# Six of the eight passes' inputs turned by VectorE blocks and SBUF transfers instead of by TensorE

## The chip, the cores and the metric

One NeuronCore of a Trainium2 chip runs the whole program. The metric is the device time of one execution in microseconds; the median of three runs stands for a kernel. TensorE (PE), VectorE (DVE), ScalarE (ACT), GpSimd (POOL) and SyncE (SP) each run their own instructions in order and meet at semaphores. SP issues all of the kernel's DMA transfers.

## What is computed

```python
# x: 4 x 512 tokens x 512
x = x + 0.5 * L0_ffn(layernorm(x))     # W1, W3: 2048 x 512; silu(x W1') * (x W3'), Hadamard, W2
x = x + L0_attn(layernorm(x))          # layernorm again, causal attention, residual
x = x + 0.5 * L0_ffn(layernorm(x))
x = x + 0.5 * L1_ffn(layernorm(x))     # ternary gate, up, down: 1408 x 512, with scales
x = x + L1_attn(layernorm(x))          # tanh(x B') C' + D * x
x = x + 0.5 * L1_ffn(layernorm(x))
```

Each feed-forward layer takes the normalised activations with the 512 features on the partitions, so the rows (tokens on the partitions) that the layernorm gives have to be transposed first: 128 tokens x 512 features at a time, a *tile*.

## The kernel before

**Passes.** The four feed-forward layers run as eight passes over half of the tokens each (two chunks of 512 tokens, eight tiles): passes 0 and 1, attention, 2 and 3 (kind A, 16 units of 128 hidden features), 4 and 5, the state-space layer, 6 and 7 (kind B, ternary, 11 units). Each pass is a row of slots, one slot for one unit. Within a slot the up products go by a seven-product scheme (p1 to p7) over sums of quarters of the input, xc_hi and xc_lo; the quarters themselves lie in xs. Every fp32 matmul is done as three with split high and low parts (`three`), or as two in the ternary passes, whose weights have no low part.

**A slot on PE** (`run`, `first_half`, `second_half`): in kind A p1, p5, p6, p2, then four down tiles, then the turns, then p7, p3, p4. In kind B p1 of slot s + 1 is done in slot s, ahead of p3 or behind it, then p4; slot s + 1 begins with p5, p6, p2, its down tiles, the turns. p6 adds onto bank BY, which `seed_y` on ACT fills; ACT may do so once DVE has read the slot before's BY in `sum_c22`. The down tiles read hid, the last block of which goes `gated_first` (DVE) -> `hid_high` (ACT) -> `low` (DVE).

**The turns** (`turn_tiles`, L997) make the input of the *next* pass in four slots of each pass: ACT normalises two tiles into xn in the slots `NORMS` (`norm_pair`, L1452; four tiles of room), one slot later PE transposes each of the two in four 128 x 128 pieces through the identity into a PSUM bank, and ACT copies the banks to xs (`turn_out`, L1300). Six passes do so (0, 2, 3, 4, 5, 6); pass 1 feeds attention and goes its own way, and pass 7 feeds nothing. Near a pass's end DVE forms the sums of the quarters (`sums`, L2053) once all eight tiles are `turned`.

**SP's order** is written out by hand. For kind A a slot issues: the next unit's up weights (`w13_load`, L579, which waits for p4 of the slot before), then a block of down weights (`w2_load`, L612). For kind B: the later parts and the low half of the next unit's up weights, which wait for p4 of the slot before; a block of down weights; then, when p6 and p2 of this slot are done, the first part of the unit after it.

**DVE's order** in a slot of kind B (`ternary_slot`, L2338): a down tile added to y (`add_tile`), `seed_z`, further down tiles and the items of `extra`, then `sum_c22` (waits for ACT's `seed_w`, hence for p7), `gated_second`, `gated_first` (waits for p4), two `hid_low`.

## Time and profile before

| | |
|---|---|
| median of 3 runs | 1706.19 us (1705.47 to 1707.06) |
| span of the profiled execution | 1703.6 us |
| PE busy | 1694.7 us, 99% |
| DVE, ACT, POOL busy | 1154.4, 830.3, 125.5 us |
| granted clock | 0.9 or more of full speed in all 40 slices |
| chain that ended last | PE 94% |
| DMA | 344.56 MB, 97341 packets |

The profiled execution's only time is its span, 2.6 us under the median of the timed runs: what lies around the program is not in it. A slot is best cut at the starts of ACT's `seed_y` (L1423), one in each unit; times within a slot of kind B are counted below from the moment at which p4 of the slot before is done, which SP's first weight load of the slot marks.

### The profile page before, as it was taken

The numbers are of one execution on the slowest core, as the hardware profiler recorded it, in microseconds if no ns is written. First come the engines' busy times: TensorE is split into PE (matmuls) and PEld (weight loads), VectorE is DVE, ScalarE is ACT, GpSimd is POOL, SyncE is SP. The second block draws the span as 40 slices with busy tenths as digits, with TensorE's granted clock in tenths as the row PEclk, the third lists the DMA queues.
The fourth block names the chain that finished last, engine by engine and source line by source line (L and its number), as shares of the span: only waits on it lengthen the run. The fifth ranks groups of instructions, "written<-read, shape, count | busy, mean of one in ns | idle before, by whom it ended". The sixth has DMA issues, their size and how long they took to land.

```text
span 1703.6 us, 21742 instructions
## 1 busy us (share of the span) xinstructions
PE 1694.7 (99%) x7707; PEld 1401.8 (82%) x7707; DVE 1154.4 (68%) x1808; ACT 830.3 (49%) x1359; POOL 125.5 (7%) x185
## 2 busy tenths in 40 slices
PE   9999999999999999999999999999999999999998
PEld 7788888888888888888888888888888888888887
DVE  8888678677775555754446554447768869877866
ACT  5745444465575543434223333224556556655644
POOL 1000000000012220000000000000000143200001
PEclk9999999999999999999999999999999999999999
DMA  9776665699985000253444433444666763366765
GB/s 317 266 310 247 229 258 211 236 377 369 369 333 207 1 0 1 87 191 126 153 167 167 167 142 136 167 167 146 232 215 211 273 222 112 113 242 234 257 221 213
DMA packets 97341, 344.56 MB, mean 202 GB/s; under 512 B 10192, under 2 KB 25424, under 8 KB 91856
## 3 DMA queue, kind: packets, MB, share of 16 engines
q1 hardware_dynamic: 97232, 343.14, 55.0%
q8 instruction: 65, 1.06, 0.2%
q14 instruction: 44, 0.36, 0.1%
HBM read 261.83 MB, written 81.26 MB: 201 GB/s over the span
## 4 chain that ended last, share of the span: by engine, by line
PE 94%; DVE 3%; DMA 1%; SPq 1%; issue 1%; ACT 0%; DVEq 0%; ACTq 0%
PE psum L561 35%; PE psum L563 30%; PE psum L565 27%; PE psum L857 2%; DMA x<-in_w2a 1%; SPq L705 1%; DVE xc_lo L2074 0%; DMA flat<-in_w3a 0%; DMA w<-w_kept 0%; PE psum L1134 0%; DVE att_lo L2043 0%; DVE fw_lo L2037 0%; SPq L664 0%; DVE x L2020 0%; DVE x L2123 0%
## 5 line engine op out<-in xcount | busy, mean ns | idle before, releaser
L561 PE MATMUL psum<-xc_hi,w 128*128 128x512 f32 x1544 | 604.6, 392 | 0.5 <-DVE psum L2143 0.3
L563 PE MATMUL psum<-xc_lo,w 128*128 128x512 f32 x1544 | 600.9, 389 | 0.0
L565 PE MATMUL psum<-xc_hi,w 128*128 128x512 f32 x928 | 361.3, 389 | 0.0
L561 PEld LDWEIGHTS psum<-xc_hi,w 128*128 128x128 f32 x1544 | 289.8, 188 | 64.4 <-DVE psum L2143 1.6
L563 PEld LDWEIGHTS psum<-xc_lo,w 128*128 128x128 f32 x1544 | 289.9, 188 | 58.8
L561 PE MATMUL psum<-w,hid 128*128 128x512 f32 x864 | 337.5, 391 | 0.0
L565 PE MATMUL psum<-w,hid 128*128 128x512 f32 x864 | 336.4, 389 | 0.0
L2107 DVE TENSOR_TENSOR x<-psum,x 128x512 f32<-128x512 f32 x256 | 173.0, 687 | 148.3 <-PE psum L565 147.7
L563 PE MATMUL psum<-w,hid 128*128 128x512 f32 x544 | 211.7, 389 | 0.0
L565 PEld LDWEIGHTS psum<-xc_hi,w 128*128 128x128 f32 x928 | 174.2, 188 | 36.7
L2131 DVE TENSOR_TENSOR hid<-sg,hid 128x512 fp32r<-128x512 f32 x212 | 144.3, 691 | 85.2 <-ACT hid L1450 83.3
L561 PEld LDWEIGHTS psum<-w,hid 128*128 128x128 f32 x864 | 162.2, 188 | 36.1 <-DVE x L2107 2.7
L565 PEld LDWEIGHTS psum<-w,hid 128*128 128x128 f32 x864 | 162.2, 188 | 33.9
L1480 ACT ACTIVATE psum<-psum 128x512 f32<-128x512 f32 x108 | 62.9, 582 | 237.6 <-PE psum L565 172.4
L1450 ACT ACTIVATE hid<-sg 128x512 fp32r<-128x512 f32 x204 | 125.6, 627 | 105.1 <-DVE sg L2156 51.9
L2147 DVE TENSOR_TENSOR sg<-psum,sg 128x512 f32<-128x512 f32 x104 | 71.6, 688 | 91.1 <-ACT psum L1480 90.7
L563 PEld LDWEIGHTS psum<-w,hid 128*128 128x128 f32 x544 | 102.2, 188 | 20.4
L2143 DVE TENSOR_TENSOR psum<-psum,sg 128x512 f32<-128x512 f32 x104 | 72.2, 694 | 43.8 <-PE psum L565 36.9
L1423 ACT ACTIVATE psum<-psum 128x512 f32<-128x512 f32 x108 | 62.8, 581 | 79.9 <-PE psum L565 54.7
L1884 POOL TENSOR_SCALAR var_eps<-meanvar 128x4 f32<-128x4 f32 x24 | 7.0, 290 | 1242.1 <-DVE meanvar L1988 865.1
L1472 ACT ACTIVATE sg<-psum 128x512 f32<-128x512 f32 x64 | 38.0, 593 | 89.2 <-PE psum L565 89.2
L1298 ACT ACTIVATE xn<-x,shift,rstd 128x512 f32<-128x512 f32 x88 | 65.7, 807 | 13.0 <-POOL shift L1887 9.9
(177 smaller groups left out, 2030.1 us busy)
## 6 DMA issues: line engine op xcount, KB each, us to landing
w<-w_kept SPq DMA_DIRECT2D x93, 896.0 KB, 6.6
w<-w_kept SPq DMA_DIRECT2D x130, 512.0 KB, 7.1
w<-w_kept SPq DMA_DIRECT2D x57, 640.0 KB, 4.4
w_kept<-w SPq DMA_DIRECT2D x16, 1792.0 KB, 7.3
w<-w_kept SPq DMA_DIRECT2D x93, 256.0 KB, 4.5
w_kept<-prep SPq DMA_DIRECT2D x12, 1792.0 KB, 7.6
w_kept<-w SPq DMA_DIRECT2D x16, 512.0 KB, 6.3
w_kept<-prep SPq DMA_DIRECT2D x12, 512.0 KB, 8.9
```

Of the source, the lines that this page charges most:

```text
L561: pe.matmul(out, a_hi, b_hi, start=start, stop=False, skip_group_check=onto)
L563: last = pe.matmul(out, a_hi, b_lo, start=False, stop=stop and zero == "a", skip_group_check=onto)
L565: last = pe.matmul(out, a_lo, b_hi, start=False, stop=stop, skip_group_check=onto)
L1298: return copy(out, x[:, i, :], AF.Identity, bias=shift[:, i:i + 1], scale=rstd[:, i:i + 1])
L1423: copy(bank(BY), bank(BX), AF.Copy).then_inc(y_seeded, 1)
L1450: copy(hid_of(u, c)[:, 0, :], own(u) if c else sg[:, 0, :], AF.Copy).then_inc(hid_hi_ready, 1)
L1472: copy(sg[:, 0, :], bank(BX), AF.Silu, scale=gate_scale(ps, s)).then_inc(c11_read, 1)
L1480: copy(bank(BW), bank(BY), AF.Copy).then_inc(w_seeded, 1)
L2107: tt(at_x, b, at_x, ALU.add).then_inc(added, 1)
L2131: tt(h[:, 1, :], source, h[:, 0, :], ALU.subtract).then_inc(hid_ready, 1)
L2143: tt(bank(BZ), bank(BY), own(u), ALU.add).then_inc(z_seeded, 1)
L2147: tt(own(u), bank(BY), own(u), ALU.add).then_inc(c22_ready, 1)
```

## The change

In passes 0, 2, 3, 4, 5 and 6 (`SWAPPED`) PE's turns and ACT's copies are gone. ACT still normalises two tiles a slot, now into two tiles' room. DVE transposes each tile's 32 x 32 blocks into `swap` (`swap_pair`), the two tiles of a pair interleaved token by token. SP then moves the blocks to their partitions in xs with 16 transfers (`turn_load`), each of 32 partitions x 4 x 64 elements (32 KB in 128 pieces of 256 bytes). The other half of xn is `swap`, so a pair's transposes wait until the pair before has landed (`turn_in`). The interleaving leaves the tokens of the up products in another order; ACT's `hid_high` and DVE's `low` undo it by reading their source with a stride of two elements in the passes that are fed in this way (1, 3, 4, 5, 7). xs holds its quarters in another order, and the sums of the next pass wait for `turn_in` in place of `turned`. In pass 6 these sums are dealt out otherwise over slots 8 and 9, and the four pairs are normalised in slots 4, 5, 6, 7 instead of 4, 4, 5, 6.

```diff
-FIRST_SUMS, LAST_SUMS = {8: 0, 9: 2}, {8: 1, 9: 3}
+FIRST_SUMS = {5: {8: (0,), 9: (2,)}, 7: {9: (1,)}}
+LAST_SUMS = {5: {8: (1,), 9: (3,)}, 7: {8: (0,), 9: (2, 3)}}
-NORMS = {4: (3, 4, 5, 6), 5: (4, 5, 6, 7), 6: (4, 4, 5, 6), 7: ()}
+NORMS = {4: (3, 4, 5, 6), 5: (4, 5, 6, 7), 6: (4, 5, 6, 7), 7: ()}
+SWAPPED = (0, 2, 3, 4, 5, 6)
+BLOCK = 32
+LANDED = 16 * 16
-TURNS = {4: (4, 5, 6, 7), 5: (5, 6, 7, 8), 6: (4, 5, 6, 7), 7: ()}
...
+        swap = at("swap", [P, P // BLOCK, KD, BLOCK, 2], F32, "xn", 4 * KIB)
...
+        def in_pairs(tile, no):
+            return tile.rearrange("p (h t i) -> p h i t", h=2, i=2) if paired(no) else tile
...
+            def turn_load(ps, k):
+                c, cols = k // 2, k % 2 * 2 * P
+                sp.wait_ge(swapped, swaps_before(ps) + 2 * k + 2)
+                if ps.kind == "B" and k == 0:
+                    sp.wait_ge(c22_read, ps.u0 + 3)
+                if ps.kind == "B" and c:
+                    sp.wait_ge(down_ready, ps.downs[4][-1][2] + 1)
+                for a in range(P // BLOCK):
+                    at = slice(cols + a * 2 * BLOCK, cols + (a + 1) * 2 * BLOCK)
+                    for b in range(P // BLOCK):
+                        sp.dma_start(xs[b * BLOCK:(b + 1) * BLOCK, 2 * c:2 * c + 2, :, at].rearrange("p h k t -> p (h k) t"),
+                                     swap[a * BLOCK:(a + 1) * BLOCK, b, :, :, :].rearrange("p k j i -> p k (j i)")).then_inc(turn_in[ps.no], 16)
...
+                if s in passes[0].norms:
+                    turn_load(passes[0], passes[0].norms.index(s))
...
+                    if ps.kind == "B" and s - 1 in ps.norms:
+                        turn_load(ps, ps.norms.index(s - 1))
                     if s + 1 < ps.n:
                         w2_load(ps.w2_0 + s, W2_BASE[ps.kind] + s)
                     if early and not late_low:
                         w13_low_load(ps.v0 + s + 1, W13_BASE[ps.kind] + s + 1)
+                    if ps.kind == "A" and ps.no in SWAPPED and s in ps.norms:
+                        turn_load(ps, ps.norms.index(s))
...
             def turn_tiles(ps, s):
-                for n, tile in ps.turns[s]:
-                    if ps.no == BEFORE_T - 1:
...
-                    else:
-                        bank_free("n", n)
-                        pe.wait_ge(xn_ready, n + 1)
-                        turn(xn[:, tile % 4, :], plan.bank["n", n]).then_inc(turn_ready, 1)
...
             def norm_pair(ps, k):
...
-                    if tile >= TT:
-                        act.wait_ge(turn_ready, first + tile - TT + 1)
+                    if k:
+                        act.wait_ge(swapped, swaps_before(ps) + tile - 1)
                         if ps.no == BEFORE_S - 1:
-                            act.wait_ge(skip_done, tile - TT + 1)
+                            act.wait_ge(skip_done, tile - 1)
...
+            def swap_pair(ps, k):
+                for j in range(2):
+                    dve.wait_ge(xn_ready, plan.norm_base[ps.no] + 2 * k + j + 1)
+                    if k:
+                        dve.wait_ge(turn_in[ps.no], k * LANDED)
+                    nc.vector.transpose(swap[:, :, :, :, j], xn[:, j, :].rearrange("p (k b t) -> p b k t", k=KD, b=P // BLOCK)
+                                        ).then_inc(swapped, 1)
...
+                if s in ps.norms:
+                    swap_pair(ps, ps.norms.index(s))
                 sum_c22(u)
                 gated(ps, s)
```

**PE, pass 5, a turn slot.** Two down matmuls, the eight pieces of the turn, the first of p7. Before:

```order
L565 MATMUL psum<-w_54,hid 128x512
L857 MATMUL psum<-ident,xn 128x128 x8
L561 MATMUL psum<-xc_hi,w_53 128x512
L563 MATMUL psum<-xc_lo,w_53 128x512
L561 MATMUL psum<-xc_hi,w_53 128x512
```

After the change such a group stands in none of the 24 slots of the six passes; p7 follows the down tiles.

**DVE, pass 4, slots 4 and 5** (y<-psum are the down tiles, sg<-psum,sg is `sum_c22`, then the two `gated` and the two `hid_low`). Before:

```order
L2111 COPY y<-psum 128x512 [waits down_ready] x3
L2147 TENSOR_TENSOR sg<-psum,sg 128x512 [waits w_seeded]
L2156 SCALAR_TENSOR_TENSOR sg<-sg,small 128x512 [waits c22_ready,c12_read]
L2163 SCALAR_TENSOR_TENSOR sg<-psum,small,sg 128x512 [waits p4_done,c11_read]
L2131 TENSOR_TENSOR hid<-sg,hid 128x512 [waits hid_hi_ready] x2
L2114 TENSOR_TENSOR y<-psum,y 128x512 [waits added,down_ready]
L2143 TENSOR_TENSOR psum<-psum,sg 128x512 [waits c12_read,p5_kept,p6_done]
```

After:

```order
L2160 COPY y<-psum 128x512 [waits down_ready] x3
L2126 STREAM_TRANSPOSE swap<-xn 128x512 [waits turn_in4,xn_ready] x2
L2197 TENSOR_TENSOR sg<-psum,sg 128x512 [waits w_seeded]
L2206 SCALAR_TENSOR_TENSOR sg<-sg,small 128x512 [waits c22_ready,c12_read]
L2213 SCALAR_TENSOR_TENSOR sg<-psum,small,sg 128x512 [waits p4_done,c11_read]
L2180 TENSOR_TENSOR hid<-sg,hid 128x512 [waits hid_hi_ready] x2
L2163 TENSOR_TENSOR y<-psum,y 128x512 [waits added,down_ready]
```

The two transposes, with the wait for the transfers of the pair before, stand ahead of `sum_c22`, the `gated` and the `hid_low` of the same slot.

**SP, pass 4, slots 5 and 6** (128x1792 is the low half of the next up weights, 128x1024 from w_54 a down block, 128x1024, 128x512 and 128x256 to w_53 the parts of the high half). Before:

```order
L609 DMA w_53<-w_kept 128x1792 [waits w13_lo_in1]
L623 DMA w_54<-w_kept 128x1024 [waits down_ready]
L577 DMA w_53<-w_kept 128x1024 [waits p2_done,p6_done]
L577 DMA w_53<-w_kept 128x512 [waits p4_done]
L577 DMA w_53<-w_kept 128x256
L609 DMA w_53<-w_kept 128x1792 [waits w13_lo_in0]
```

After:

```order
L638 DMA w_53<-w_kept 128x1792 [waits w13_lo_in1]
L751 DMA xs<-swap 32x4x64 [waits down_ready,swapped]
L751 DMA xs<-swap 32x4x64 x15
L652 DMA w_54<-w_kept 128x1024 [waits down_ready]
L606 DMA w_53<-w_kept 128x1024 [waits p2_done,p6_done]
L606 DMA w_53<-w_kept 128x512 [waits p4_done]
L606 DMA w_53<-w_kept 128x256
L638 DMA w_53<-w_kept 128x1792 [waits w13_lo_in0]
```

The 16 transfers of the pair that DVE turned in the slot before stand behind the low half of the up weights and ahead of the down block. In kind A they stand at the end of the same slot, behind both.

## Rows read from the trace of the kernel before

**Rows 1.** The page: busy time (share of the span) xinstructions; shares of the chain.

```profile
PE 1694.7 (99%) x7707; PEld 1401.8 (82%) x7707; DVE 1154.4 (68%) x1808; ACT 830.3 (49%) x1359; POOL 125.5 (7%) x185
...
PE 94%; DVE 3%; DMA 1%; SPq 1%; issue 1%; ACT 0%; DVEq 0%; ACTq 0%
```

**Rows 2.** Windows: stretch, length, each engine's busy us (instructions), PEclk, DMA share, GB/s.

```profile
1260.85:1271.74 10.89, 10.89 (x53) 9.09 (x52) 6.69 (x11) 5.26 (x9) 0.00 (x0) 1.00 0.61 218
1271.74:1281.72 9.98, 9.98 (x45) 8.26 (x44) 8.74 (x13) 4.18 (x8) 0.00 (x0) 1.00 0.67 233
1050.44:1066.33 15.89, 15.89 (x75) 13.22 (x74) 6.83 (x10) 5.22 (x10) 0.00 (x0) 1.00 0.42 150
1066.33:1081.29 14.96, 14.96 (x67) 12.39 (x66) 6.83 (x10) 4.13 (x8) 0.00 (x0) 1.00 0.43 157
192.95:208.89 15.94, 15.94 (x75) 13.14 (x74) 10.61 (x17) 7.32 (x12) 0.00 (x0) 1.00 0.56 209
```

**Rows 3.** Timeline of PE, pass 4, slots 5 and 6: start, us, what, count.

```profile
1246.14 1.04 PE L857 MATMUL psum<-ident,xn 128*128 128x128 f32 x8
...
1251.82 0.39 PE L563 MATMUL psum<-xc_lo,w 128*128 128x512 f32 x1
...
1253.41 0.39 PE L561 MATMUL psum<-w,hid 128*128 128x512 f32 x1
```

**Rows 4.** Timeline of DVE, pass 4, slot 6, with idle time before and its releaser.

```profile
1250.96 0.75 DVE L2163 SCALAR_TENSOR_TENSOR sg<-psum,small,sg 128x512 f32<-128x512 f32 x1 [0.42 <-PE psum L563]
1252.41 1.29 DVE L2131 TENSOR_TENSOR hid<-sg,hid 128x512 fp32r<-128x512 f32 x2 [0.70 <-ACT hid L1450]
...
1257.24 0.69 DVE L2114 TENSOR_TENSOR y<-psum,y 128x512 f32<-128x512 f32 x1 [0.22 <-PE psum L565]
1259.65 0.69 DVE L2147 TENSOR_TENSOR sg<-psum,sg 128x512 f32<-128x512 f32 x1 [1.72 <-ACT psum L1480]
```

**Rows 5.** Timeline of ACT, pass 4, the seed of bank BY.

```profile
1249.98 0.58 ACT L1423 ACTIVATE psum<-psum 128x512 f32<-128x512 f32 x1 [0.23 <-PE psum L563]
```

**Rows 6.** Timeline of SP's issues, pass 4, slot 6, and the low half's landing.

```profile
1250.88 0.79 SPq L577 DMA_DIRECT2D w<-w_kept  x2
...
1252.19 0.43 SPq L623 DMA_DIRECT2D w<-w_kept  x1
...
L609 SPq DMA_DIRECT2D w<-w_kept x1: 430/430/430, 1251.7 to 1251.7; - x1
...
DMA to landing us min/median/max: 6.4/6.4/6.4
```

**Rows 7.** SP's densest rows of issues: timeline of the start, and line L705.

```profile
1.64 1.37 SPq L664 DMA_DIRECT2D x<-in_w2a  x3
3.05 4.34 SPq L671 DMA_DIRECT2D att_raw<-in_att_w  x8
...
L705 SPq DMA_DIRECT2D w_scratch<-stage x8: 377/1284/5267, 22.6 to 61.3; - x8
```

**Rows 8.** DMA issues of 67.5 to 73 us: KB each, median us to landing.

```profile
w_scratch<-x SPq DMA_DIRECT2D x2, 256.0 KB, 2.3
```

**Rows 9.** DVE work on 512 and on 1024 elements: page; all of one line.

```profile
L2131 DVE TENSOR_TENSOR hid<-sg,hid 128x512 fp32r<-128x512 f32 x212 | 144.3, 691 | 85.2 <-ACT hid L1450 83.3
...
L2068 DVE TENSOR_TENSOR xn<-xs x8: 1211/1216/1226, 60.1 to 1564.7; 128x1024 f32<-128x1024 f32 x8
```

**Rows 10.** Pass 3, a turn-free slot: DVE's last down tile, SP's issues, a landing.

```profile
1075.85 0.69 DVE L2107 TENSOR_TENSOR x<-psum,x 128x512 f32<-128x512 f32 x1 [0.67 <-PE psum L565]
...
1079.92 0.80 SPq L577 DMA_DIRECT2D w<-w_kept  x2
...
DMA to landing us min/median/max: 6.8/6.8/6.8
```

**Rows 11.** Timeline of DVE, pass 0: between the two hid_low.

```profile
178.17 0.69 DVE L2131 TENSOR_TENSOR hid<-sg,hid 128x512 fp32r<-128x512 f32 x1 [1.15 <-ACT hid L1450]
```

**Rows 12.** Windows: pass 5, slot 4.

```profile
1340.26:1351.70 11.44, 11.44 (x52) 9.49 (x51) 9.40 (x16) 5.59 (x9) 1.76 (x2) 1.00 0.49 164
```

More of the change, by code:

```diff
@@ L110, in __init__ @@
         self.own, self.other, self.spare = [], [], 2
-        self.turn = PT
+        self.turn = self.norm = PT
+        self.norm_base = {}
         for no in range(len(PASSES)):
@@ L157, in add_pass @@
                         ps.turns[s].append((n, n))
-            elif no < len(PASSES) - 1 and s in ps.turn_slots:
-                for j in range(2):
-                    self.use(("n", self.turn), 3)
-                    ps.turns[s].append((self.turn, 2 * ps.turn_slots.index(s) + j))
-                    self.turn += 1
         if kind == "B":
@@ L193, in state_space @@
         self.s_unit, self.s_w2 = self.u, self.w2
-        self.s_downs, self.s_turn = [[] for _ in range(CH)], self.turn
+        self.s_downs, self.s_turn, self.s_norm = [[] for _ in range(CH)], self.turn, self.norm
+        self.norm += PT
         self.uses += -self.uses % 4
@@ L444, in converted, with all_turned, swaps_before, paired @@
             return conv_base(no) + CONVERSIONS[no].index(m) + 1
-        def turns_before(no):
-            return PT * (no + 1 + (no >= BEFORE_S))
+        def all_turned(no):
+            if no == "S":
+                return turn_in[BEFORE_S - 1], PT // 2 * LANDED
+            if no - 1 in SWAPPED and no != BEFORE_S:
+                return turn_in[no - 1], PT // 2 * LANDED
+            return turned, PT * {0: 1, BEFORE_T: 2, BEFORE_S: 3}[no]
+        def swaps_before(ps):
+            return PT * SWAPPED.index(ps.no)
+        def paired(no):
+            return no not in (0, BEFORE_T, BEFORE_S)
+        def of_unit(u):
+            return next(ps.no for ps in passes if ps.u0 <= u < ps.u0 + ps.n)
+        def in_pairs(tile, no):
+            return tile.rearrange("p (h t i) -> p h i t", h=2, i=2) if paired(no) else tile
+        def by_tile(tile, no):
+            return tile.rearrange("p (h i t) -> p h i t", h=2, i=2) if paired(no) else tile
         def hid_of(u, c):
@@ L1533, in up_slot @@
                     norm_pair(ps, ps.norms.index(s))
-                if ps.no != BEFORE_T - 1:
-                    for n, tile in ps.turns[s]:
-                        if tile == 0:
-                            act.wait_ge(xc_ready, conv_base(ps.no) + 7)
-                        turn_out(n, tile, plan.bank["n", n])
                 seed_w(u)
@@ L1617, in ternary_slot @@
                         norm_pair(ps, k)
-                for n, tile in ps.turns[s]:
-                    turn_out(n, tile, plan.bank["n", n])
                 if s == ps.n - 2:
@@ L1941, in _ @@
             pool.wait_ge(skip_in, 16)
-            for n, tile in (tt for tiles in passes[BEFORE_S - 1].turns for tt in tiles):
+            for tile in range(PT):
                 if tile == 2:
                     chunk()
-                pool.wait_ge(turn_ready, n + 1)
-                skip(xn[:, tile % TT, :], x[:, tile, :], xn[:, tile % TT, :])
+                pool.wait_ge(swapped, swaps_before(passes[BEFORE_S - 1]) + tile + 1)
+                skip(xn[:, tile % 2, :], x[:, tile, :], xn[:, tile % 2, :])
             chunk()
@@ L2249, in up_slot @@
                     hid_low(u, 1)
+                    if swapping and ps.no == 0:
+                        swap_pair(ps, ps.norms.index(s))
                     hid_low(u, 0)
@@ L2344, in ternary_slot @@
                     return
-                if follower(ps) and s in FIRST_SUMS:
-                    sums(follower(ps), FIRST_SUMS[s])
+                if follower(ps):
+                    for step in FIRST_SUMS[ps.no + 1].get(s, ()):
+                        sums(follower(ps), step)
                 behind = bool(ps.downs[s]) and s not in ps.open
@@ L2359, in ternary_slot @@
                     extra(ps, s, k + 1)
-                if follower(ps) and s in LAST_SUMS:
-                    sums(follower(ps), LAST_SUMS[s])
+                if follower(ps):
+                    for step in LAST_SUMS[ps.no + 1].get(s, ()):
+                        sums(follower(ps), step)
+                if s in ps.norms:
+                    swap_pair(ps, ps.norms.index(s))
                 sum_c22(u)
@@ L2398, in state_low @@
             def state_low(c, j):
-                low(("s", c, j), hid[:, 2 * (c % 2) + j, :, :], sg[:, j, :])
+                low(("s", c, j), hid[:, 2 * (c % 2) + j, :, :], sg[:, j, :], "S" if c < 2 else BEFORE_S)
             def state_x_low(c, i):
```

72 lines of the change are left out of this document (42 added, 30 removed).

## The prediction

> **What bounds the kernel now.** I read the page first: PE is busy for 1694.7 of 1703.6 us and makes 94% of the chain that ended last [rows 1]. So the span falls by the time that PE is spared, as long as nothing else makes PE wait, and it grows by each wait that PE is given. Then I cut the passes into slots. A turn slot of kind B takes 10.89 us and the next, turn-free one 9.98; in kind A it is 15.89 against 14.96, with 15.94 in pass 0, and PE is busy all through each, at full clock [rows 2]. All the slack is on the other engines: DVE has 6.7 to 8.7 us of work in a slot of kind B of about 10 [rows 2]. Last I followed one turn-free stretch of kind B event by event, counted from the end of the former p4 (1250.88, when SP issues [rows 6]): DVE's last down tile ends at 7.05 and `sum_c22` starts at 8.77, having waited for ACT's copy behind p7 [rows 4]; p6 of this slot starts at 0.94 and the down tiles at 2.53 [rows 3].
>
> **What goes.** Eight transposes stand in each turn slot, 24 slots in all (192 of the 320 on xn). They last 1.04 us by the row [rows 3], but overlap with what follows; the slots say 10.89 - 9.98 = 0.91 and 15.89 - 14.96 = 0.93. 24 x 0.91 = **21.8 us** less PE work. ACT's 48 copies to xs go too; ACT is no bound, so they count nothing.
>
> **What comes, on DVE.** 48 block transposes of 512 elements a partition, two in a slot. No row shows one. Ordinary work on 512 elements takes 0.69 us, two in a row 1.29 [rows 9, 4]; work on 1024 elements takes 1.22 [rows 9]. The lower end fits an engine that still passes one element a cycle; I take 1.3 us a pair, range 1.2 to 2.4. In the first turn slot of a pass they fill the idle stretch from 7.05 to 8.35. p7 comes 0.91 earlier than now, so `sum_c22` could have started at 7.86: 0.5 us late. What tolerates that: behind the swap stand `sum_c22`, two `gated` and ACT's `hid_high`, and the low part that the next down tiles need. In the trace `gated_first` starts at 0.08, the pair of low parts at 1.53, the first of them is done at 2.2, and the down tiles at 2.53 [rows 3, 4]. So `gated_first` may be 0.3 late. With a slot of 9.97 the swap must end by **9.0**, since `sum_c22` and `gated_second` take 0.65 each behind it; p6, which needs `sum_c22` and a seed of 0.58 [rows 5], gives the later limit of 9.6. Ending at 8.35 costs nothing.
> The Trainium skill, page "VectorE: DVE Perf Modes", section "The three transpose paths", gives VectorE 311 ns for 128 x 128 bf16. Were four of these one of ours, a transpose would last 1.24 us and the time would come out as in the third rival; no run here shows it yet.
>
> **What comes, on SP.** 16 issues a pair, 384 in all. Start to start an issue in a dense row takes 0.42 to 0.47 us [rows 6, 7], eight loads at the start average 0.55 [rows 7], and issues of 512 pieces each against a full queue have a median of 1.28 [rows 7]. Ours have 128 pieces. I take **0.50**, range 0.43 to 0.65, so the last is issued 7.5 us after the first. A transfer of 256 KB (in 512 pieces) on an idle queue lands 2.3 us after its issue [rows 8], one of 896 KB 6.4 us [rows 6]. By bytes alone that is 0.64 us for 100 KB, and ours of 32 KB would land after 0.9; by pieces ours is a quarter of the former. I take 1.8, nearer to the row that is nearest to it, range 0.9 to 2.3. From the first issue to the last landing: **9.3 us**.
>
> **Kind A.** DVE's last down tile ends 11.6 into the slot (1076.54 against 1064.96, one slot of 14.96 before the issue at 1079.92) [rows 10]; with the swap 12.9. SP then issues until 20.9, where the next unit's weights were due at 15.0. Their low half lands 0.84 + 6.8 us after their first issue [rows 6, 10], at 28.5, and PE wants it at 29.9. Covered by 1.4 us, and the pair has landed (22.2) long before the next swap. In pass 0 the swap stands in an idle gap of 1.15 us between the two `hid_low` [rows 11], and what it delays on SP (the store of weights, the next raw loads) has a slot of slack. So the three passes of kind A keep their gain of 12 x 0.91.
>
> **Kind B.** Here the slot is as short as the transfers are long. SP issues the pair in the slot after its swap, behind the up weights: first issue at 9.97 + 1.3 = 11.3 from the start of the first swap slot. It lands at 20.6. DVE, which stands before the second swap since 9.97 + 7.05 = 17.0, waits until then; all that is queued behind it on DVE (`sum_c22`, `gated`, `hid_low`, the next down tiles) waits too, and ACT's seed and PE's p6 and down tiles for these. The swap ends at 21.9 instead of 9.97 + 9.0 = 19.0: PE loses **2.9**. SP issues the second pair at 21.95, it lands at 31.25, the swap ends at 32.55; with the loss before, the limit is 19.94 + 2.9 + 9.0 = 31.8: **0.7**. The third pair must wait for the weights of its slot, which starts at 32.8: issue 34.1, landing 43.4, end 44.7, limit 29.9 + 3.6 + 9.0 = 42.5: **2.2**. Together 5.8 a pass, three passes 17.4. The fourth pair lands before its sums are due, but in pass 6 `sums` stands at the end of the very slot in which it is sent: 0.6 more. In pass 4 the second swap slot is a longer one: 1.8 less. In pass 5 DVE is already busy for 9.4 of 11.44 us in slot 4, with an even fuller slot before [rows 12]: 0.8 more. Sum **17.0 us**.
> The delayed transfers behind: the down block of the slot is issued at 9.3 instead of 1.3 and is wanted at 9.97 + 2.5 plus the loss; with a landing of some 3.5 us that is just covered. The first part of the unit after next goes at 9.8 instead of 2.8 and is wanted a slot later. The low half lands 6.4 us after its issue [rows 6], at 7.2, so the first of our transfers queue behind it, but the last is issued later than that.
>
> **The reads with a stride** in `hid_high` and `low`. No row shows one. From below they cost nothing (the same 512 elements), from above as much as 1024 elements, 0.53 more each [rows 9]. I take nothing.
>
> **Sum.** -21.8 + 17.0 = -4.8 us. On the profiled span 1703.6 that is 1698.8; on the median 1706.19 it is **1701.4**.
>
> **Rivals.**
> *1. Nearly all hidden.* Issues of 0.42 and a landing of 1.4 put the loop of swap, issues and landing (1.3 + 6.3 + 1.4 = 9.0) below the slot. The first pair then lands at 19.0 and costs 1.3, the third as much, some 7 in the three passes: 1706.2 - 21.8 + 7 = 1691. For it: the two closest issues are 0.42 apart [rows 6]. Against: those behind them are 0.47 apart [rows 6, 7].
> *2. The sixteen go out more slowly, slower than before.* Place: SP's queue. At 0.65 an issue the loop is 9.75 + 1.8 + 1.3 = 12.9 against a slot of 9.97: about 3 to 5 us in three or four slots a pass, 35 in all; and in kind A the next weights go out at 23.3, land at 31.0 instead of 29.9, 1.1 us in eight slots, 9 more. -21.8 + 35 + 9 = +22: 1728. It turns slower than before from 0.55 an issue on (each 0.01 costs 1 us). For it: the eight loads at the start and the 1.28 [rows 7]; against it: those moved 256 KB each through a full queue. The same happens if 128 pieces of 256 bytes take more than 0.55 us to drain, though they are issued faster.
> The Trainium skill, page "DMA: Bandwidth & Descriptors", section "Specifications", says that transfers of under 512 bytes a piece are read, modified and written; its section "Why small descriptors are slow (HBM only)" exempts SBUF to SBUF. Our pieces have 256 bytes. By the first rule this rival is likelier, by the second the forecast stands; no row here has such pieces.
> *3. DVE's work is dearer.* Transposes of 1.2 us each lengthen every loop by 1.1: some 7 us more, 1708. Reads with a stride of twice the price delay `hid_high` and `low` by 1 us in each of some 30 slots of kind B, where 0.3 is free: 20 us, 1721.
> *4. The change doesn't do what it says.* Ruled out by the order: the transposes are gone from the 24 slots.
>
> **Chances.** Forecast (the loop is a little longer than the slot) 0.52, its own range 1694 to 1707; nearly all hidden 0.12; slow queue 0.22; dearer DVE 0.14. The range from 1689 to 1722 leaves out the better end of the first rival and the worse end of the second. A measurement of this kernel can tell 0.2%, 3.4 us, from no change. Faster by more (under 1702.8): most of the forecast's cases and the first rival, 0.53. Within: 0.19. Slower: 0.28.
>
> **What would show it.** Turn slots of kind A at 14.96 us, no PE gap. In kind B, DVE idle before the second, third and fourth STREAM_TRANSPOSE with a transfer to xs as its releaser, 3 to 4 us in the second; PE gaps of 1 to 3 us before p6 or the down tiles in the slots after. SP's sixteen 0.50 apart. Wrong if the transposes last over 0.75, if the issues average over 0.55, or if SP's down block becomes the last to come.

## The result, and the profile after

The changed kernel takes **1741.7 us** (median of 4 runs, 1739.8 to 1753.7) against 1706.6 for the kernel before beside it (1705.5 to 1707.4): a ratio of 1.022, 95% interval 1.019 to 1.025, so 35 us **slower**. The profiled run has a span of 1737.6 us, 34.0 more than that of before. The forecast said 1701.4, within 1689 to 1722. The sign was wrong and the time lies outside the range.

The page of the changed kernel, its busy time and its chain, which answer to [rows 1]:

```profile
PE 1693.3 (97%) x7515; PEld 1389.9 (80%) x7515; DVE 1187.7 (68%) x1856; ACT 808.2 (47%) x1311; POOL 127.1 (7%) x185
...
PE 78%; SPq 10%; DMA 5%; DVE 3%; issue 2%; ACT 1%; ACTq 0%; DVEq 0%
PE psum L590 29%; PE psum L592 25%; PE psum L594 22%; SPq L751 9%; DMA w<-w_kept 3%; PE psum L909 1%; DMA xs<-swap 1%; PE psum L878 1%; DVE swap L2126 1%; SPq L606 1%; DMA mix_in_raw<-mix_raw 1%; DMA w_scratch<-stage 0%; DVE x L2156 0%; SPq
```

The 192 transposes are gone from PE, and yet it is busy for only 1.4 us less. The chain, which ran on PE for 94%, now runs for 9% through SP's queue, at the line of the sixteen transfers (L751).

Six windows, each from the first to the last slot of a pass that the change moves (passes 0, 2, 3, 4, 5 and 6, the last one to its end), show where it went. First the kernel before, then the changed one; the columns are those of [rows 2].

```profile
145.15:223.91 78.76, 78.76 (x363) 64.86 (x362) 54.55 (x85) 40.58 (x61) 1.86 (x4) 1.00 0.56 206
759.85:823.33 63.48, 63.48 (x297) 52.86 (x296) 28.62 (x44) 25.07 (x43) 1.60 (x4) 1.00 0.41 150
1002.85:1066.33 63.48, 63.48 (x297) 52.86 (x296) 28.62 (x44) 25.08 (x43) 1.59 (x4) 1.00 0.41 149
1226.40:1271.74 45.34, 45.34 (x217) 37.85 (x216) 26.90 (x41) 25.29 (x42) 0.00 (x0) 1.00 0.60 209
1340.26:1395.44 55.18, 55.17 (x260) 45.81 (x259) 39.54 (x62) 31.06 (x51) 23.50 (x21) 1.00 0.61 215
1505.74:1589.26 83.52, 83.52 (x386) 69.32 (x385) 60.98 (x90) 51.19 (x82) 1.59 (x4) 1.00 0.58 204
```

```profile
144.60:223.14 78.54, 76.31 (x334) 62.12 (x333) 58.47 (x91) 36.25 (x52) 1.87 (x4) 1.00 0.65 217
759.38:825.35 65.97, 62.25 (x265) 50.48 (x264) 32.27 (x51) 20.71 (x34) 1.59 (x4) 0.97 0.56 178
1004.87:1069.12 64.25, 60.66 (x265) 49.32 (x264) 32.40 (x51) 20.96 (x34) 1.59 (x4) 1.00 0.57 181
1229.30:1281.40 52.10, 45.83 (x185) 36.59 (x184) 30.30 (x47) 21.12 (x35) 0.00 (x0) 0.93 0.65 200
1350.02:1416.21 66.19, 56.83 (x228) 44.55 (x227) 49.54 (x70) 26.91 (x44) 26.82 (x22) 0.92 0.62 194
1526.51:1623.52 97.01, 86.64 (x354) 69.32 (x353) 65.63 (x98) 46.57 (x75) 1.59 (x4) 0.93 0.61 197
```

By length the differences are -0.2, +2.5, +0.8, +6.8, +11.0 and +13.5: **+3.0 in kind A and +31.3 in kind B**, together the 34 us. Each pass was to shorten by 3.6 (four slots by 0.91), so the losses are 14 us in kind A and 42 in kind B, where the forecast had none and 17. The windows show two things that make up most of these 56 us: PE is idle (35.5 us in the six windows, length less PE's busy time, against 0.01 before) in 21 gaps, and the granted clock is at 0.92 to 0.97 in four of them, which is some 14 us (below). Some 7 us are left. Half of that is what each gap costs beyond its idle time: PE's matmuls last 0.39 us and start 0.23 apart, so 0.16 of overlap is lost in each gap, 3.4 us in all. The other half was not broken down.

**The loop on the swap buffer.** SP's queue in pass 4, over two turn slots (start, us, what, count):

```profile
1244.55 11.03 SPq L751 DMA_DIRECT2D xs<-swap  x16
1255.62 0.59 SPq L652 DMA_DIRECT2D w<-w_kept  x1
1256.31 1.32 SPq L606 DMA_DIRECT2D w<-w_kept  x3
1257.68 0.42 SPq L638 DMA_DIRECT2D w<-w_kept  x1
1258.29 10.58 SPq L751 DMA_DIRECT2D xs<-swap  x16
1268.91 0.59 SPq L652 DMA_DIRECT2D w<-w_kept  x1
```

SP hardly rests here. The sixteen take 10.6 to 11.0 us, 0.645 apart, and the five weight loads fit exactly between two rows of them: 13.3 us of work in a slot that had 9.97. The last transfer lands 1.9 us after its issue, at 1270.20, the swap starts at 1270.29. From swap to swap (1256.95 to 1270.29) that is 1.3 us of VectorE, 10.0 from the first issue to the last, 1.9 for the last landing and 0.1 between them, and the slot has the same 13.3 us. What the tile `swap` says for the whole kernel:

```profile
L751 SPq DMA_DIRECT2D xs<-swap x384: 585/601/1877, 145.8 to 1591.7; - x192
L2126 DVE STREAM_TRANSPOSE swap<-xn x48: 669/684/715, 144.5 to 1581.2; 128x512 f32<-128x512 f32 x48
its engine sat idle before it (us, times) until:
  DMA xs<-swap: 35.2, 11
...
DMA to landing us min/median/max: 1.9/2.0/7.2
```

The block transpose is as cheap as I took it (684 ns, two in 1.3 us). The wait for the transfers, 35.2 us in 11 places, is the whole of the mechanism forecast, only larger.

**The weights of kind A.** In pass 3 (window of 1004 to 1070) PE's idle time has another releaser, the weights that SP issued behind the sixteen:

```profile
L590 PE MATMUL psum<-xc_hi,w 128*128 128x512 f32 x59 | 23.2, 394 | 3.6 <-DMA w<-w_kept 3.6
```

**The clock.** After some of the gaps PE runs slowly. PE's timeline behind a gap of pass 4, and two windows, the gap and what follows it:

```profile
1259.56 0.50 PE L590 MATMUL psum<-xc_hi,w 128*128 128x512 f32 x1 [1.85 <-ACT psum L1467]
...
1261.55 0.63 PE L590 MATMUL psum<-xc_hi,w 128*128 128x512 f32 x1
1261.98 0.63 PE L592 MATMUL psum<-xc_lo,w 128*128 128x512 f32 x1
...
1264.25 0.40 PE L594 MATMUL psum<-w,hid 128*128 128x512 f32 x1
```

```profile
1257.32:1259.56 2.24, 0.39 (x2) 0.00 (x0) 2.14 (x4) 0.58 (x1) 0.00 (x0) 1.00 0.96 382
1260.70:1264.01 3.31, 3.31 (x9) 2.63 (x8) 1.29 (x2) 2.76 (x6) 0.00 (x0) 0.52 1.03 353
```

PE was idle for 1.85 us; 1.1 us after it resumed, the granted clock fell to 0.52, the level of 1.2 GHz, and matmuls stood 0.43 us apart instead of 0.23, for some 3 us. Seven of the 21 gaps are followed by such a stretch (one in pass 2, two each in passes 4, 5 and 6), with 58 matmuls of 0.63 us in all: 58 x 0.2 = 11.6 us. With the matmuls at the edges of the stretches, and the first ones behind the three longest gaps (4.4 to 4.8 us, in which the clock fell before PE resumed), it is **some 14 us** that no term of the forecast held. Before, no turn slot has one.

### The profile page after: what moved, and what is told of

It is laid out like the page before. It is cut to its first block, busy times and chain, and to the rows that moved or that the text cites. A ratio compares the mean times of both kernels' runs of the same rounds, so it can differ in the third digit from the quotient of the medians.

```text
span 1737.6 us, 21736 instructions
## 1 busy us (share of the span) xinstructions
PE 1693.3 (97%) x7515; PEld 1389.9 (80%) x7515; DVE 1187.7 (68%) x1856; ACT 808.2 (47%) x1311; POOL 127.1 (7%) x185
## 4 chain that ended last, share of the span: by engine, by line
PE 78%; SPq 10%; DMA 5%; DVE 3%; issue 2%; ACT 1%; ACTq 0%; DVEq 0%
PE psum L590 29%; PE psum L592 25%; PE psum L594 22%; SPq L751 9%; DMA w<-w_kept 3%; PE psum L909 1%; DMA xs<-swap 1%; PE psum L878 1%; DVE swap L2126 1%; SPq L606 1%; DMA mix_in_raw<-mix_raw 1%; DMA w_scratch<-stage 0%; DVE x L2156 0%; SPq L687 0%; DVE sg L2197 0%
## 5 line engine op out<-in xcount | busy, mean ns | idle before, releaser
L2180 DVE TENSOR_TENSOR hid<-sg,hid 128x512 fp32r<-128x512 f32 x212 | 152.3, 728 | 92.0 <-ACT hid L1495 89.3
L590 PEld LDWEIGHTS psum<-w,hid 128*128 128x128 f32 x864 | 164.7, 191 | 42.7 <-DVE x L2156 5.5
L594 PEld LDWEIGHTS psum<-w,hid 128*128 128x128 f32 x864 | 164.1, 190 | 34.7
L1495 ACT ACTIVATE hid<-sg 128x512 fp32r<-128x512 f32 x204 | 129.6, 647 | 101.0 <-DVE sg L2206 52.1
L592 PEld LDWEIGHTS psum<-w,hid 128*128 128x128 f32 x544 | 102.2, 188 | 20.5
```

The costliest lines, as they stand in the source:

```text
L590: pe.matmul(out, a_hi, b_hi, start=start, stop=False, skip_group_check=onto)
L592: last = pe.matmul(out, a_hi, b_lo, start=False, stop=stop and zero == "a", skip_group_check=onto)
L594: last = pe.matmul(out, a_lo, b_hi, start=False, stop=stop, skip_group_check=onto)
L1495: copy(by_tile(hid_of(u, c)[:, 0, :], no), in_pairs(own(u) if c else sg[:, 0, :], no), AF.Copy).then_inc(hid_hi_ready, 1)
L2180: tt(by_tile(h[:, 1, :], no), in_pairs(source, no), by_tile(h[:, 0, :], no), ALU.subtract).then_inc(hid_ready, 1)
```

## The experiments

The theory after this reading: **SP's issues are the bottleneck**. Rivals: the bytes or the small pieces; VectorE's added work or the reads with a stride; the order on the queue.

### The price of an issue, alone

```diff
+            price(0, [(to[b * 32:(b + 1) * 32, :, :, a * 64:(a + 1) * 64].rearrange("p h k t -> p (h k) t"),
+                       price_from[a * 32:(a + 1) * 32, b, :, :]) for a in range(4) for b in range(4)])
...
+            price(4, [(price_dram[0], price_from[:, :, :, :].rearrange("p b k t -> p (b k t)"))])
```

> The kernel before, with groups of transfers behind its last store, when nothing else runs; each group is waited for before the next. Group 1: sixteen as in the change (32 partitions x 4 pieces of 256 B). 2: sixteen of 32 partitions x one piece of 1 KB. 3: eight of 128 partitions x 4 pieces of 256 B. 4: sixteen of 32 partitions x one piece of 256 B. 5: 512 KB to DRAM in one transfer. 6: back in sixteen of 32 KB. 7: the pair to DRAM in four transfers with pieces of 256 B, and back in one. 8: group 1 issued by ACT. 9: four of them issued by POOL. My theory, that SP's price is one of the issue itself and not of a crowded queue: group 1 is 0.60 to 0.65 us start to start here too, as it was 0.645 in the changed kernel, and its last lands 1.9 us after its issue. The rival, that the other transfers under way slowed the sixteen: 0.45 to 0.50 here. If the number of pieces makes the price, groups 2 and 4 are at 0.40 to 0.45 and group 3 at 1.2 (a dense row of transfers with 512 pieces had a median of 1.28 in the kernel before); if it is the count of dimensions, groups 2 and 4 are cheap and group 3 is at 0.65; if it is the number of issues alone, all are at 0.6.

SP's timeline behind the last store: groups 1 to 4 (source and destination in SBUF), then group 6 (from DRAM); then ACT's and POOL's.

```profile
1703.51 10.40 SPq L818 DMA_DIRECT2D price_to<-xn  x16
1715.25 10.07 SPq L818 DMA_DIRECT2D price_to<-xn  x16
1726.63 5.54 SPq L818 DMA_DIRECT2D price_to<-xn  x8
1733.88 10.08 SPq L818 DMA_DIRECT2D price_to<-xn  x16
1747.80 7.45 SPq L818 DMA_DIRECT2D price_to<-price_dram  x16
...
1769.73 10.48 ACTq L1895 DMA_DIRECT2D price_to<-xn  x16
1781.82 2.54 POOL L2011 DMA_DIRECT2D price_to<-xn  x4 [82.76 <-DMA price_to<-xn]
```

On an idle chip the sixteen take 10.4 us, as in the kernel, so no crowding made them slow. Pieces don't matter: 128 pieces of 256 B (0.645 start to start), 32 of 1 KB (0.63), 32 of 256 B (0.63), 512 of 256 B (0.69). The number of dimensions doesn't either. What matters is that both ends lie in SBUF: the same 32 KB in the same pieces from **DRAM** go out 0.475 apart. Every row from which I had taken 0.50 (0.42 to 0.47, [rows 6, 7]) was a load from DRAM. The landings of 1.9 us (256 B) and 1.8 (1 KB) show no extra price for small pieces between SBUF and SBUF. The Trainium skill, page "DMA: Bandwidth & Descriptors", exempts SBUF to SBUF from that price in "Why small descriptors are slow (HBM only)"; the run agrees with it, and not with the unrestricted rule of its "Specifications".

With one end in DRAM the pieces do matter. Groups 5 and 7: the pair to DRAM in one store (pieces of 4 KB), then in four (pieces of 256 B), and back in one load of 512 pieces.

```profile
1745.14 0.33 SPq L818 DMA_DIRECT2D price_dram<-xn  x1
...
1756.64 5.64 SPq L818 DMA_DIRECT2D price_dram<-xn  x4
1765.96 0.60 SPq L818 DMA_DIRECT2D price_to<-price_dram  x1
```

The one store has landed 2.6 us after its issue. Of the four the last two took SP 2.0 us each to issue, and the load that waits for them goes out 9.3 us after the first. So the short price of a transfer from or to DRAM holds for few or long pieces, not for many short ones.

### The same bytes in fewer transfers

```diff
-                for a in range(P // BLOCK):
-                    for b in range(P // BLOCK):
-                        sp.dma_start(xs[b * BLOCK:(b + 1) * BLOCK, 2 * c:2 * c + 2, :, at].rearrange("p h k t -> p (h k) t"),
-                                     swap[a * BLOCK:(a + 1) * BLOCK, b, :, :, :].rearrange("p k j i -> p k (j i)")).then_inc(turn_in[ps.no], 16)
+                sp.dma_start(xs[:, 2 * c:2 * c + 2, :, cols:cols + 2 * P].rearrange("p h k t -> p (h k) t"),
+                             swap[:, :, :, :, :].rearrange("p b k j i -> p b (k j i)"))
```

> The changed kernel, where a pair goes in one transfer of 512 KB (each partition's data stay in their partition, so the blocks are not where the reference wants them and the output is another) in place of sixteen. Bytes, waits, transposes and reads with a stride are the same. If the sixteen issues are the cause of the loss: SP has 5 issues in a slot again, the pair lands some 4 to 5 us after its issue, the loop is about 6.5 us against a slot of 9.97, and the time is 1706.2 - 21.8 = 1684, at most 1690; no drop of the granted clock in the passes of kind B. If VectorE's transposes, the reads with a stride or the bytes are the cause, it stays above 1715, near the 1741.7 of the change.

> The changed kernel with the same bytes and pieces in eight transfers a pair of 64 partitions (256 pieces of 256 B each; they stay in their partitions, so the output is another than the reference's). If the number of issues sets the price (0.645 each): 8 x 0.645 + 1.9 + 1.3 = 8.4 us of loop against a slot of 9.97, first pair landed at 11.3 + 7.1 = 18.4, swap ends at 19.7 against 19.0: under 1 us a pass, in all 1685 to 1690. If the number of pieces sets it, eight issues cost 1.2 each, as much as sixteen of 0.645, and the time is 1735 to 1742.

> The changed kernel with the same bytes and pieces in four transfers a pair of 128 partitions (512 pieces of 256 B each; they stay in their partitions, so the output is another than the reference's). If the number of issues sets the price: 4 x 0.645 + about 2.5 + 1.3 = 6.4 us of loop, everything is hidden and the time is 1684 to 1687. If it is the pieces, four issues at 1.3 to 2.4 each keep the loop at 8 to 13 us and the time lies between 1700 and 1742.

| transfers a pair | us | ratio to before (95%) |
|---|---|---|
| 16 (the change) | 1741.7 | 1.022 (1.019 to 1.025) |
| 8 | 1705.2 | 0.999 (0.998 to 1.000) |
| 4 | 1700.0 | 0.996 (0.995 to 0.998) |
| 1 | 1698.2 | 0.995 (0.993 to 0.997) |

Bytes, waits and VectorE's work are equal in all four, and the pieces are equal in the first three. From sixteen to eight 36 us vanish: **the number of issues is the cause of most of the change's loss**. One thing differs besides: with eight, four and one the blocks stay in their partitions (so the output is another). On the idle chip an issue that does so (group 3, 0.69) was no cheaper than one that crosses (group 1, 0.645), so this doesn't explain the 36 us. But all three missed the 1684 to 1690 expected. With one transfer the twelve turn slots of kind A are at 14.96 to 15.04, as forecast, and what is left is in kind B. The tile `swap` of that run:

```profile
  DMA xs<-swap: 14.3, 7
...
DMA to landing us min/median/max: 3.2/6.3/9.8
```

One issue costs SP nothing now, and still VectorE waits 14.3 us for landings. In kind B the transfer is issued right behind the low half of the next up weights. In pass 4 this (896 KB) lands in 7.2 to 7.5 us and the pair some 1.5 us behind it, 8.3 to 9.1 after its own issue (7.3 to 9.8 in all of kind B). The granted clock, which the expectation had at full, still falls once, in pass 5 (0.97 over its slots 4 to 8).

### The order on the queue

```diff
-                                 ps.u0 + s - 1 if ps.kind == "B" and s else None, not early,
+                                 ps.u0 + s - 1 if ps.kind == "B" and s else None, not early and not paired_slot,
...
                         turn_load(ps, ps.norms.index(s - 1))
+                        w13_low_load(ps.v0 + s + 1, W13_BASE[ps.kind] + s + 1)
```

> The run with one transfer a pair (output another than the reference's, for the same reason), with that transfer ahead of the low half of the next up weights in kind B instead of behind it; nothing else moves. With the low half ahead the pair landed 8.4 us after its issue, 1.5 us after the low half's landing, and VectorE waited 2.7 us for it at the second swap. If that order is what was left of the loss (1698.2 against 1684.4), the pair lands 3 to 4 us after its issue and the time is 1684 to 1689. If it was VectorE's added work (1.3 us a slot) or the reads with a stride, the time stays at 1696 to 1699.

> The changed kernel with its sixteen transfers ahead of the low half of the next up weights in kind B, same output. SP's work in such a slot stays 16 x 0.645 and five loads, some 13.3 us against a slot of 9.97. If SP's own time is the bound, the slots stay at 13.3 and the time at 1737 to 1745. If the landing behind the low half was a part of it, the loop shortens by the 0.5 us of one issue only, 3 x 3 x 0.5 = 4 us: 1737. If the late low half itself becomes what PE waits for, it is slower: over 1745.

With one transfer, ahead of the low half: **1689.4 us**, ratio 0.989 (0.988 to 0.991), 9 to 10 us less than behind it and 0.4 over the range of its expectation. The tile `swap` has no wait for a transfer left, and a turn slot of pass 4 has the length and PE share of a turn-free one of before; the second window is slot 5 of pass 5.

```profile
DMA to landing us min/median/max: 3.2/4.4/5.1
```

```profile
1228.84:1238.81 9.97, 9.97 (x45) 8.26 (x44) 7.77 (x13) 5.65 (x9) 0.00 (x0) 1.00 0.89 306
1340.19:1352.07 11.88, 11.22 (x47) 8.22 (x45) 11.01 (x18) 5.66 (x10) 6.74 (x9) 1.00 0.72 247
```

So VectorE's 1.3 us in a slot do cost nothing in passes 4 and 6. The rest over 1684.4 is mostly pass 5, where VectorE is busy for 11.0 of 11.88 us: slots 4 and 5 are 1.2 and 0.8 us longer than the same slots before, and slots 4 to 8 together take 55.7 us against 55.2, where 3.6 less were due. So pass 5 loses some 4 us.

With sixteen transfers the same move wins nothing: 1749.9, ratio 1.025 (1.023 to 1.026), where the change has 1.019 to 1.025; a real loss against the change is not shown. The time is that of the last outcome of the expectation (over 1745), its cause isn't. The page (idle before the first matmuls, and before the down tiles):

```profile
L590 PE MATMUL psum<-xc_hi,w 128*128 128x512 f32 x1544 | 610.8, 396 | 35.4 <-ACT psum L1469 26.0 <-DMA w<-w_kept 8.7 <-DVE psum L2195 0.3
...
L590 PE MATMUL psum<-w,hid 128*128 128x512 f32 x864 | 340.8, 394 | 7.5 <-DMA w<-w_kept 4.2 <-DVE x L2158 1.6 <-DVE hid L2182 1.6
```

Of the 8.7 us before the first matmuls nearly all is kind A's wait for weights, which this edit doesn't touch (the same groups of PE in the trace, pass by pass). In kind B PE hardly waits for the low half, which goes out 10 us later. It waits 4.2 us for the down block that now stands behind it, 2.8 of them at one place in pass 5. The swap still waits 33.9 us for its transfers, 35.2 in the change.

### The reads with a stride

```diff
-            return no not in (0, BEFORE_T, BEFORE_S)
+            return False
```

> The run with one transfer a pair, ahead of the low half (1689.4), with the reads and writes with a stride in the splitting of the hidden values made straight ones (output another than the reference's, as there). By the forecast's term they cost nothing: 1688 to 1690. Their rows say 728 ns against 691 on VectorE and 647 against 627 on ACT; if these 40 and 20 ns each count in full on the path of kind B, where each slot has two, the time falls by 2 to 3 us more, to 1686.

1689.5 us (1688.3 to 1690.6) against 1689.4: nothing, as forecast. The reads are 40 ns dearer (728 against 691), and no wait that PE sees goes through them.

### Another engine issues

```diff
+POOL_SHARE = {0: 16, 2: 16, 3: 16, 4: 12, 5: 6, 6: 12}
...
+                    turn_load(pool, passes[no], k, blocks[:pool_share(passes[no])], turn_in_pool)
```

> The changed kernel with the sixteen transfers of a pair spread over two queues, same output: in kind A POOL issues all sixteen, in kind B twelve (in pass 5 six, behind its own work on the pair) and SP the other ones, ahead of the low half of the next up weights. If SP's queue is the cause of the loss: POOL issues at 0.55 us start to start (four of them did in the run with the priced transfers), so its twelve go from 8.35 to 15.0 and have landed at 16.9, SP's four from 11.3 + 1.5 to 15.4 and landed at 17.3, all about when VectorE comes to the next swap (17.0); kind A has its weights in time: 1706.2 - 21.8 = 1684, with pass 5 (where POOL has 6 us of other work a pair) and what the queue adds 1684 to 1694. If the landing behind the weights or VectorE's own load is what counts, it stays at 1698 or above, as with one transfer a pair. If POOL's transfers are dearer beside other work than alone, over 1706.

1739.3 us, ratio 1.019 (1.017 to 1.020): a clear miss. Half of it held: with SP free of the sixteen, all eight turn slots of passes 2 and 3 are at 14.96. In kind B only 3 us were won (212.2 us in the three windows, 215.3 in the change), and in pass 0 it was lost (three slots of 16.6 to 19.0). POOL's and SP's issues in pass 4:

```profile
1237.21 3.08 SPq L631 DMA_DIRECT2D xs<-swap  x4
1240.34 0.60 SPq L669 DMA_DIRECT2D w<-w_kept  x1
...
1235.75 6.59 POOL L631 DMA_DIRECT2D xs<-swap  x12 [4.07 <-DVE swap L2165]
```

Twelve at 0.55 end at 1242.3, but SP, which needs only 3.1 us for its four, sends the low half at 1240.34, ahead of POOL's last three. POOL's transfers issued before 1240 landed after 1.8 to 3.2 us, the last three after 5.0, 5.9 and 6.1. It is so in all turn slots of kind B: 70 of POOL's transfers were issued with no low half under way and landed after 1.8 to 3.4 us, 50 with one under way after 2.8 to 7.2, with a median of 5.7. The low half delays their landing though it was issued on another queue. The Trainium skill, page "DMA: Bandwidth & Descriptors", section "Issuing engines are not separate DMA queues", says that all issuing engines' transfers run on the same 16 DMA engines and that a second issuer saves only the time of issuing; this run agrees. Its section "Queues, rings and completion order" says two things that bear on this: the engines serve the queues in turn, by which 32 KB would hardly wait behind 896; and the semaphore increment that tells of a landing comes only after every earlier write of that engine, on whichever queue. The measured 5.0 to 6.1 us fit the second; whether the data themselves came earlier no run shows. The lesson of the run before, that the pair must go ahead of the low half, I had kept on one queue only.

### Through DRAM, with eight issues

```diff
+            for a in range(P // BLOCK):
+                nc.gpsimd.dma_start(swap_kept[k, a].rearrange("(b q) n -> q b n", b=4),
+                                    swap[a * BLOCK:(a + 1) * BLOCK, :, :, :, :].rearrange("q b k j i -> q b (k j i)"))
...
+                sp.dma_start(xs[:, 2 * c:2 * c + 2, :, at].rearrange("p h k t -> p (h k) t"),
+                             swap_kept[k, a].rearrange("p (k t) -> p k t", k=4))
```

> Same output as the change, the blocks moved through DRAM: POOL stores a pair in four transfers right behind VectorE's swap (pieces of 1 KB), SP brings it back in four (its loads from DRAM were 0.475 us start to start where those from SBUF took 0.645), ahead of the low half of the next up weights in kind B, and VectorE's next swap waits for the stores alone. If the count of SP's issues and the place ahead of the low half are the whole cause: stores issued from 8.9 to 11.1 in the swap's slot and landed at 14, loads landed at about 18, nothing waits for them; kind A at 14.96 a slot, kind B at 9.97, and 1706.2 - 21.8 + 2 to 6 for pass 5 = 1686 to 1691. If SP, which waits for the stores, makes the low half too late, or the doubled bytes crowd the weights, kind B's slots are at 11 to 12 us: 1695 to 1710.

1709.8 us, ratio 1.002 (1.001 to 1.003): 32 us better than the change, and not what was expected. All twelve slots of kind A keep their 0.9, and so do the first three of passes 4 and 6. But the last turn slots of each pass of kind B, or the one behind them, lose, one of them 7.7 us. The stores land after 2.3 to 4.2 us at the start of a pass and after 6.5 to 7.2 at its end, and PE waits for the down weights (page):

```profile
L601 PE MATMUL psum<-w,hid 128*128 128x512 f32 x864 | 339.4, 393 | 10.2 <-DMA w<-w_kept 9.8 <-DVE y L2203 0.4
```

That fits the second alternative of the expectation, that the doubled bytes are more than kind B's slots can carry; no run took the bytes alone away. SP's loads were dearer than expected too: of 512 pieces each, they are issued 0.57 to 0.68 us apart in their dense rows and not 0.475. And the end is 4.5 us longer: the last store's issue ends at 1699.9, and the span ends at 1707.2; in the kernel before it is 1700.8 and 1703.6. In the trace POOL's closing drain lasts 9.6 us here, 1.8 before. The only difference on POOL is that it issues transfers; the run with twelve of them on POOL had a drain of 7.6 us and an end 2.1 us longer.

### Kind A alone, three ways

```diff
-SWAPPED = (0, 2, 3, 4, 5, 6)
+SWAPPED = (0, 2, 3)
```

> Same output. Only kind A is turned by VectorE, exactly as in the change (sixteen transfers behind the swap, the next up weights behind them). Read from the slots of the changed kernel: pass 0 -0.3 and +0.6 in pass 1, pass 2 +2.5, pass 3 +0.8: 1706.2 + 3.6 = 1710, range 1707 to 1713, so kind A loses too and the other 32 us of the change's +35.5 are kind B's. By the forecast it would be 1706.2 - 10.9 = 1695.

> Same output. Only kind A is turned by VectorE, with the sixteen transfers of the change, but four of them go ahead of the next up weights and twelve behind them and the down weights. SP's own time is not the bound in kind A (16 x 0.645 + 2.4 = 12.7 us of 15); the order is. If the late up weights were the loss of kind A (they went out at 23.3 instead of 15.0 in its slot), they are 0.5 us late now and the last transfer has landed at about 17.5 + 12 x 0.645 + 1.9 = 27.1, 0.5 us behind the start of the next swap: 1695 to 1698. If the swap's wait for that landing takes their place, the four passes' middle slots lengthen by 1 to 2 us: 1700 to 1706.

> Same output. Only the three passes of kind A are turned by VectorE (kind B by PE, as in the kernel before), and their blocks go through DRAM, all issued by SP: four stores behind the swap (0.645 each, done 2.6 us later, ahead of the next up weights, so these are 0.5 us late), and four loads in the next slot behind the weights. In the run through DRAM all twelve such slots were at 14.96 to 15.05 us, but POOL's drain made the end 4.3 us longer; here POOL issues nothing. If the cause is understood: 12 x 0.91 less, 1706.2 - 10.9 = 1695, range 1694 to 1698. If SP's four stores are already too much ahead of the weights: 1700 and above.

| kind A alone | us | ratio (95%) | who PE waits for |
|---|---|---|---|
| as in the change | 1715.2 | 1.005 (1.004 to 1.007) | DMA w<-w_kept, 10.4 us |
| 4 transfers ahead of the weights, 12 behind | 1730.7 | 1.014 (1.013 to 1.016) | VectorE, which waits for its transfers |
| through DRAM, all issued by SP | **1696.3** | **0.994 (0.993 to 0.995)** | DMA w<-w_kept, 1.3 us, outside the turn slots |

The releasers of the first two, from PE's groups of the first and the tile `swap` of the second:

```profile
L595 PE MATMUL psum<-xc_hi,w 128*128 128x512 f32 x1544 | 605.5, 392 | 12.4 <-DMA w<-w_kept 10.4 <-DVE psum L2209 0.9 <-ACT psum L1473 0.6
```

```profile
  DMA xs<-swap: 37.1, 9
```

The first run lies 2 us over the range of its expectation, the second 25 us over, the third inside. The sixteen fit into a slot of kind A by their sum (12.7 of 15 us), but either order has a victim: ahead of the weights they make PE wait for these; behind them they can make VectorE wait for the landing. In passes 2 and 3 the second order is by far the cheaper: their four turn slots take 61.0 and 61.5 us in the second run, 67.5 and 64.3 in the first, 63.5 before and 59.8 with nothing late. So with sixteen transfers it wins 4.5 us there, and nearly all that the second run loses it loses in pass 0 (slots of 26.9, 21.5 and 26.2). There SP's queue also holds stores with waits of their own, and the twelve of the pair swapped at 145.4 stand behind one of them: they go out from 159.35 on, and VectorE waits 9.7 us for them. This order in passes 2 and 3 alone, with pass 0 left out, was not run. The third has neither victim, since the next swap waits for the stores alone. A turn slot of pass 0 and one of pass 3, and the tile `swap`, before whose transposes VectorE never waits for a transfer:

```profile
174.86:189.89 15.03, 15.03 (x67) 12.31 (x66) 11.75 (x20) 7.64 (x11) 0.00 (x0) 1.00 0.80 272
1026.65:1041.61 14.96, 14.96 (x67) 12.39 (x66) 8.07 (x13) 5.60 (x9) 0.00 (x0) 1.00 0.73 229
```

```profile
L751 SPq DMA_DIRECT2D swap_kept<-swap x48: 318/440/1426, 146.1 to 1039.4; - x48
L2155 DVE STREAM_TRANSPOSE swap<-xn x24: 669/686/706, 144.8 to 1037.4; 128x512 f32<-128x512 f32 x24
```

It is 0.6% **faster than the kernel before** with the same output, 10.8 us by the medians where 10.9 were forecast for kind A, and the best of all versions here that compute the reference.

## Why the prediction was wrong, point by point

- **What goes, 21.8 us: right.** Wherever nothing else is late, a turn slot shortens by 0.89 to 0.93.
- **VectorE's transposes, 1.3 us a pair: right** (48 x 684 ns). The 1.24 us for one that four times the figure of the Trainium skill would have given (page "VectorE: DVE Perf Modes", section "The three transpose paths") is not what the trace shows: 0.68.
- **That they cost nothing in kind B: right** in passes 4 and 6, but the 0.8 us for pass 5 were some 4.
- **The reads with a stride, nothing: right.**
- **SP's issues, 0.50: this is the step that failed.** They are 0.645, at the upper end of the range given. It was the sum's most sensitive term (I had written 1 us for each 0.01) and the value was taken from the densest rows of loads, though the section itself had rows of 0.55 and above. The rows were of another kind: their source was DRAM. No row of before has both ends in SBUF, and a value without its own row should have been weighed nearer to the middle of its range than to the cheapest rows; with 0.55 the sum would have given about 1706 and no sign at all. By the forecast's own 1 us for each 0.01 the 0.145 are 14.5 of the 40 us between forecast and result. The rest, by estimate, is what the sum didn't hold: kind A's 14 and the clock's 12 in kind B, both of which hang on the same price: with eight transfers a pair kind A loses nothing (turn slots of 14.96 to 15.06), and two of the seven slow stretches are left.
- **Landing 1.8: right for a single one** (1.9), wrong for those behind the low half. The forecast said that the last of them is issued late enough, which holds only while there are sixteen: with one transfer the order alone costs 9 us.
- **Kind B, 17.0 us: the mechanism was right** (swap, issues, landing, swap; VectorE idle in front of the second, third and fourth swap), **the size was not: 42**. The second rival had the right place and price for an issue, and 35 us. What both lacked is the clock: six of the seven slow stretches, some 12 us, lie in kind B, and each costs 1.6 to 2.9 us on top of the gap before it.
- **Kind A, nothing lost: wrong, 14 us** (19 in the run of kind A alone: 8 us slower where 10.9 were to be gained). The cover of 1.4 us was worked out right, and it was used up by 16 x 0.145 = 2.3 us. The rival had 9. Pass 0's "slot of slack" wasn't there either: three slots in a row were 0.8, 1.9 and 0.7 us too long, with `mix_in_raw<-mix_raw` on the chain.
- **The chances.** Slower had 0.28. From 0.55 on it was slower, and nearly half of the range that I gave for an issue (0.43 to 0.65) lies above that; 0.22 for this rival was too little by the text's own numbers.
- **The third rival's sum** was too small by its own terms: 1.1 us more in three loops of three passes are 9.9, not 7. It played no part.

What stays open: the 14 us of the clock are counted from the trace and weren't taken away by a run of their own. What kind B would give with sixteen transfers in an order that hurts no one isn't known; no such order was found there, while in passes 2 and 3 the split order comes near it.

## What to carry to other kernels

Many small transfers in place of PE work are a load on the queue that issues them: multiply their number by the price of an issue of the same kind (source and destination), and compare the sum with what the queue has free in the shortest slot. A queue is ordered, and here the landings of one queue also waited for a large transfer on another: whatever a loop waits for has to go ahead of the large transfers that nobody needs yet. A stall of PE can cost more than its length: behind seven of the 21 gaps here the granted clock was low, for 1.6 to 2.9 us more each.

## What the runs showed of the hardware that I had not expected

- An issue from SBUF to SBUF costs SP 0.63 to 0.69 us start to start for 8 to 128 KB, whatever the pieces; ACT 0.65, POOL 0.55. One from DRAM costs 0.475 with 128 pieces, and 0.57 to 0.68 with 512 in the run through DRAM. The stores to DRAM of the last version (pieces of 1 KB) took 0.44 at the median, those with 512 pieces of 256 B on the idle chip up to 2.0.
- A transfer on POOL's queue issued 0.4 us after 896 KB on SP's took 5.0 us to land; those issued before it took 1.8 to 3.2. Over all of kind B the medians are 5.7 and 2.2.
- A kernel in which POOL issues transfers ended with a drain of 7.6 to 9.6 us on POOL instead of 1.8, and a span 2.1 to 4.5 us longer behind the last store's issue.
- After a PE gap of 1.85 us the granted clock fell to 0.52 (1.2 GHz) for some 3 us, though it had been 1.00 in the gap and 1.1 us beyond it.
